# Second FFN: four passes over the input rows on another engine, and the row transposes later in a group

## The chip, the cores and the metric

The kernel runs on one core of a Trainium2 chip. The metric is device time in microseconds (us), the median over several executions. A profiled execution gives the trace: for each engine (PE for matmuls, DVE for vector work, ACT for activations and copies, POOL for GpSimd, SP for DMA issue) every instruction with its start and duration, counted from the first instruction of the execution.

## The reference

Sixteen batches of 256 rows of width 256 go through two layers. Each layer adds an attention-like part and a feed-forward part to the rows, each on layer-normalised rows. The change touches only the last of the four, an FFN with simulated 4-bit numbers:

```python
def fake_quant_nvfp4(x, global_scale):        # blocks of 16 along the last axis
    amax = jnp.max(jnp.abs(xb), axis=-1, keepdims=True)
    sc8 = jnp.clip(amax / 6.0 * global_scale, 0.0, 448.0).astype(float8_e4m3fn)
    dq = sc8 / global_scale
    a = jnp.clip(jnp.abs(xb) / safe_dq, 0.0, 6.0)
    q = jnp.sign(xb) * _FP4_VALS[jnp.digitize(a, _FP4_MIDS)]
    return (q * dq).reshape(sh)
...
gate_out = nvfp4_linear(x, gate_w, s_in[0])   # both operands quantised, then a matmul
up_out = nvfp4_linear(x, up_w, s_in[0])
hidden = jax.nn.silu(gate_out) * up_out       # 1024 wide
return nvfp4_linear(hidden, down_w, s_in_down[0])
```

So both the normalised rows (256 wide) and the hidden activations (1024 wide) are scaled by block, clamped, rounded and multiplied back before a matmul.

## The kernel before, in words

The 4096 rows are 32 tiles of 128 rows (a row is a partition). The second FFN takes them in 8 groups of four tiles. Each engine has its own instruction list, written out by hand, and the engines meet in semaphores. Work on three groups is in flight at once. In one round of the DVE list, `group(g, rows)` (L2226), DVE does, in this order:

- `rows_sizes(g + 2)`: the largest value of each block of 16 of the input rows two groups ahead, from a copy `absx` that ACT made (L1930, L1932);
- `hidden_sizes(g)`: the same for the hidden activations of group g (L1959, L1961, L1930, L1932);
- `block_scales`: five small instructions on 320 columns, 64 for rows and 256 for hidden, ending in a reciprocal (L1936 to L1941). They write `inv16` (what to multiply by before rounding) and `scb` (what to multiply by after);
- the four passes over the 1024 row elements of a partition: `rows_scaled` (L1965, times `inv16`, into `xf`), `clamped` (L1973), `rounded` (L1976) and the last multiplication into `xq` (L1981), which tells `s_xq`;
- the four passes over the first half of the hidden activations (2048 elements each: L1970, L1973, L1976, L2215), and then, in turn, the second half's passes and `product` (L2223, one instruction for each half of a tile: SiLU of the gate times the up result, PSUM and SBUF in, `hh` out) for the four tiles of group g + 1.

Rounds 0 to 5 handle rows (for groups 2 to 7); round 6 and the closing group have none. The rows of groups 0 and 1 are quantised before the rounds.

PE, in `finished(i)` (L1506), first transposes the quantised rows of group i + 2 (`x_in`, L1449, into PSUM bank 0), then the hidden activations of group i (`hidden_in`, L1479, in bank 6, 0, 6, 6 for the four tiles), waiting before the second for ACT to have emptied bank 0 (`s_xqe`), and multiplies them by the down weights (`down`, L1495 and L1497). Then `ahead(i + 1)` (L1500) does gate (L1458) and up (L1467) for the four tiles of group i + 2; `up` waits for `product` to free its banks.

ACT, in its `group(i)` (L1021), does SiLU (L988), a 16-bit copy of the hidden activations (`hidden_half`, L996), then `x_out` (L980, bank 0 to `xqT`), two of the `hidden_out` copies (L1012), `tile_norm(i + 4)` for i up to 3 (six instructions, L824 to L829: normalise four tiles, make `absx` and `xb`), the other two `hidden_out` and a `result` (L1017).

POOL has nothing to do in the second FFN. Earlier it issues indirect DMAs and does two-input multiplications and additions in 32-bit floats (among them L592 and L629).

`Steps.link(ins)` in the listing lets an instruction raise a semaphore and makes the same engine wait for it, before the next instruction reads the result.

Of the kernel before, what the change touches and what calls it, by code (L numbers as in the profile page):

```python
# [7 lines left out]
ALU = mybir.AluOpType  # L8
# [6 lines left out]
I16 = mybir.dt.int16  # L15
U32 = mybir.dt.uint32

P = 128
# [44 lines left out]
def two_layers_kernel(nc, x, itok, ctxT, ctxO, mask, maskT, w_redT, wgT, W1, W2, b2,  # L63
# [46 lines left out]
    with es:  # L110
# [3 lines left out]
        def sem(name):  # L114
            return es.enter_context(nc.semaphore(name))

        def sem2(name):
            return [sem(f"{name}{h}") for h in range(2)]
# [279 lines left out]
                             "s_dn", "s_y")]  # L398
        s_h, s_gs, s_nm2, s_x4 = sem("s_h"), sem("s_gs"), sem("s_nm2"), sem("s_x4")
        s_ax, s_ah = sem("s_ax"), sem("s_ah")  # L400
        s_out = sem2("s_out")
        N_CONST = 12

# [113 lines left out]
        def _(pool):  # L517
# [100 lines left out]
            def weight_scaled(k, first=False):  # L618

                if not first:  # L620
                    pool.wait_ge(s_wp, k)
                pool.sem_inc(s_idle, 1)
                flat = wraw[:].rearrange("p n d -> p (n d)")
                src = (flat[:, 0:2 * FT * D][:, bass.ds(k * NGU, NGU)].rearrange("p (t k b) -> p t k b", t=TGU, k=BLOCK),
                       wraw[:, 2].rearrange("p (t k b) -> p t k b", t=DC, k=BLOCK)[:, :, :, bass.ds(k * BDN, BDN)])
                inv = (wblk[:, 4, 0:2 * NWB // 3][:, bass.ds(k * (NGU // BLOCK), NGU // BLOCK)].rearrange("p (t b) -> p t b", t=TGU),
                       wblk[:, 4, 2 * NWB // 3:NWB].rearrange("p (t b) -> p t b", t=DC)[:, :, bass.ds(k * BDN, BDN)])
                for to, x, m in zip((wt[:, 0:NGU], wt[:, NGU:NGU + NDN]), src, inv):
                    ins = pool.tensor_tensor(to.rearrange("p (t k b) -> p t k b", t=x.shape[1], k=BLOCK), x,  # L629
                                             m.unsqueeze(2).broadcast_to([P, m.shape[1], BLOCK, m.shape[2]]), ALU.mult)  # L630
                ins.then_inc(s_wm, 1)
# [43 lines left out]
            with pool.Else():  # L675
                pool.sem_inc(s_cv, 1)
                with pool.Fori(0, NB) as b:
                    pool.wait_ge(s_cv, b + 1)
                    pool.tensor_copy(cb[:], ctxs[:, bass.ds(b, 1), :, 0:S].rearrange("p o c s -> p (o c) s")).then_inc(s_cb, 1)
                pool.wait_ge(s_cv, NB + 1)  # L680
                weight_first()
                for k in range(1, SLOTS):
                    weight_scaled(k)


        @block.scalar
        def _(act):
# [132 lines left out]
            def tile_norm(g, g0):  # L820

                for u in range(4):
                    t = g * 4 + (u + 1)
                    ins = act.activation(x4s[g0 % 2][:, u * D:(u + 1) * D], X2[:, bass.ds(t, 1), 0:D].rearrange("p o d -> p (o d)"), ACT.Identity,  # L824
                                         bias=nm2[:, bass.ds(t, 1)], scale=rs2[:, bass.ds(t, 1)])
                ins.then_inc(s_x4, 1)
                act.wait_ge(s_x4, g + 1)
                act.activation(absx[g0 % 2], top(x4s[g0 % 2]), ACT.Abs)
                act.copy(xb[g0 % 2], top(x4s[g0 % 2])).then_inc(s_ax, 1)  # L829
# [164 lines left out]
            def hidden_half(t, u):  # L994
                act.wait_ge(s_h, 2 * t + 2)
                act.copy(hb[:, u * FF:(u + 1) * FF], upper(u)).then_inc(s_ah, 1)  # L996
# [13 lines left out]
            def hidden_out(g, u, banks=(6, 0, 6, 6)):  # L1010
                act.wait_ge(s_hT, g * 4 + (u + 1))
                act.copy(hqT[:, u % 2].rearrange("p c t -> p (c t)"), bank[banks[u]][:].bitcast(BF16)).then_inc(s_hTe, 1)  # L1012

            def result(g, k):
                act.wait_ge(s_dn, g * 4 + (2 * k + 2))
                act.wait_ge(s_out[k], g * 16 + 16)
                act.activation(yo[:, k].rearrange("p t d -> p (t d)"), bank[(1, 7)[k]][:], ACT.Copy, scale=gmx[:, 10:11]).then_inc(s_y, 2)  # L1017
# [3 lines left out]
            def group(i):  # L1021
                t = i * 4 + 4
                last = i == NGR - 2
                if i == 0:
                    x_out(1)
                silu(t, 0)
                silu(t + 1, 1)
                if i:
                    result(i - 1, 1)
                hidden_half(t, 0)  # L1030
                silu(t + 2, 2)
                hidden_half(t + 1, 1)
                silu(t + 3, 3)
                hidden_half(t + 2, 2)
                hidden_half(t + 3, 3)
                if not last:
                    x_out(i + 2)
                hidden_out(i, 0)
                hidden_out(i, 1)
                if i + 4 < NGR:  # L1040
                    tile_norm(i + 4, i + 4)
                hidden_out(i, 2)
                hidden_out(i, 3)
                result(i, 0)

            for i in range(NGR - 1):
                group(i)
# [6 lines left out]
        def _(pe):  # L1054
# [390 lines left out]
            def x_in(g):  # L1445
                pe.wait_ge(s_xq, g + 1)
                for u in range(4):
                    for c in range(DC):
                        ins = pe.transpose(bank[0][:].bitcast(BF16)[:, (u * DC + c) * P:(u * DC + c + 1) * P],  # L1449
                                           xq[g % 2][:, u, c * P:(c + 1) * P], identb[:])  # L1450
                ins.then_inc(s_xqT, 1)
# [31 lines left out]
            def down(i, u, turn=False, banks=(1, 7)):  # L1483
                pe.wait_ge(s_hTe, i * 4 + (u + 1))
                if turn:
                    hidden_in(i, 3)
                rows = banks[0] == 1
                if u == 0:
                    if rows:
                        pe.wait_ge(s_y, i * 4)  # L1490
                    else:
                        pe.wait_ge(s_h, 2 * NTILE)
                to = bank[banks[u // 2]][:, (u % 2) * D:(u % 2 + 1) * D]
                if rows:
                    pe.matmul(to, ones[:], X2[:, bass.ds(i * 4 + (u + 1), 1), 0:D].rearrange("p o d -> p (o d)"), start=True, stop=False)  # L1495
                for c in range(FT):
                    ins = pe.matmul(to, hqT[:, u % 2, c, :], dT[:, c, :], start=not rows and c == 0, stop=c == FT - 1)  # L1497
                ins.then_inc(s_dn, 1)
# [5 lines left out]
                    up(i * 4 + (4 + u), u)  # L1504

            def finished(i):  # L1506
                if i + 2 < NGR:
                    x_in(i + 2)
                hidden_in(i, 0)
                if i + 2 < NGR:  # L1510
                    pe.wait_ge(s_xqe, i + 3)
                hidden_in(i, 1)
                down(i, 0)
                hidden_in(i, 2)
                down(i, 1)
                down(i, 2, turn=True)
                down(i, 3)

# [15 lines left out]
        def _(v):  # L1534
# [422 lines left out]
            def hidden_sizes(g, steps):  # L1957
                v.wait_ge(s_ah, g * 4 + 3)
                ts(absh[:, 0:3 * FF].bitcast(I16), hb[:, 0:3 * FF].bitcast(I16), 0x7FFF, None, ALU.bitwise_and)  # L1959
                v.wait_ge(s_ah, g * 4 + 4)  # L1960
                steps.link(ts(absh[:, 3 * FF:].bitcast(I16), hb[:, 3 * FF:].bitcast(I16), 0x7FFF, None, ALU.bitwise_and))  # L1961
                halves(absh, halfh, 4, NBH // 4, big[:, hid_c], steps)
# [263 lines left out]
            def group(g, rows):  # L2226

                t = g * 4 + 4
                later = g > 0
                if rows:  # L2230
                    rows_sizes(g + 2, g + 2, st)
                hidden_sizes(g, st)
                block_scales(slice(0 if rows else NBX, NBX + NBH), st)
                if rows:
                    rows_scaled(g + 2, st)
                    rows_quantised(g + 2, st)
                hidden_scaled(0, st)
                st.need()
                clamped(hf[:, pair[0]], st)
                rounded(hf[:, pair[0]], st)  # L2240
                if later:
                    v.wait_ge(s_hT, g * 4 - 2)
                hidden_quantised(0)
                product(t, 0)
                hidden_scaled(1, st)
                product(t + 1, 1)
                st.need()
                clamped(hf[:, pair[1]], st)
                rounded(hf[:, pair[1]], st)
                product(t + 2, 2)  # L2250
                if later:
                    v.wait_ge(s_hT, g * 4)
                hidden_quantised(1)
                product(t + 3, 3)
# [109 lines left out]
```

## Time and profile before

| what | us |
|---|---|
| median of 3 runs | 712.79 (712.4 to 712.82) |
| profiled execution, device time | 713.3 |
| its span, first to last instruction | 711.1 |
| PE busy | 567.0 (80%) |
| DVE busy | 504.9 (71%) |
| ACT busy | 378.0 (53%) |
| POOL busy | 213.3 (30%) |

The busy times are shares of the whole span, over stages that differ: the second FFN is the part from about 505 us to the end. The profiled execution took 2.2 us more than its span and 0.5 us more than the median. A view by time gives, for a stretch, how long each engine worked in it; the trace in order of time gives, for each instruction, its start, its duration, its line, and in brackets how long its engine had been idle and who ended that.

### The profile page before, as it was taken

To read this page: it belongs to the slowest core of one execution; us is meant where nothing else is said; L and a number is where in the kernel's file an instruction comes from. 1 tells how busy PE (TensorE), PEld (TensorE's weight loads), DVE (VectorE), ACT (ScalarE), POOL (GpSimd) and SP (SyncE) were. 2 spreads that over 40 slices of the span, in tenths; PEclk is the share of its full clock that TensorE was granted. 3 is DMA by queue.
4 is the path that set the end of the run, shared out by engine and by line. 5 is a ranking of instruction groups with operands and counts; after the bars stand their busy time and mean duration, and the time that the engine had idled before them with its cause. 6 is when DMAs were issued, how large, how long until landed. Compare 5 with 4: busy or idle time off the path is not lost.

```text
span 711.1 us, 14550 instructions
## 1 busy us (share of the span) xinstructions
PE 567.0 (80%) x4543; PEld 417.5 (59%) x4552; DVE 504.9 (71%) x1418; ACT 378.0 (53%) x717; POOL 213.3 (30%) x243
## 2 busy tenths in 40 slices
PE   5399999609999999966899999996435865778777
PEld 3188888409998998954566666664212443345445
DVE  6358787694655566673556777663769999999987
ACT  1324443113443333324667777767675878785674
POOL 5724774514655455652222333310000000000000
PEclk9689999959999999996999999999667999998899
DMA  8873443269466655607000000000000000000001
GB/s 318 270 229 117 131 150 116 76 221 386 140 221 198 198 177 181 202 29 238 2 1 0 0 0 0 0 2 1 4 1 0 30 15 16 30 29 16 16 30 60
DMA packets 35540, 68.49 MB, mean 96 GB/s; under 512 B 5581, under 2 KB 24542, under 8 KB 34464
## 3 DMA queue, kind: packets, MB, share of 16 engines
q1 hardware_dynamic: 28816, 52.37, 22.4%
q0 software_dynamic: 5520, 13.61, 5.5%
q10 hardware_dynamic: 1152, 1.88, 0.8%
q8 instruction: 26, 0.43, 0.2%
q14 instruction: 26, 0.21, 0.1%
HBM read 53.78 MB, written 15.80 MB: 98 GB/s over the span
## 4 chain that ended last, share of the span: by engine, by line
PE 45%; DVE 22%; ACT 13%; issue 8%; DMA 7%; SPq 3%; POOL 2%; DVEq 0%; POOLq 0%; ACTq 0%
PE quad L1118 10%; PE quad L1183 5%; DVE hh L2223 5%; ACT nPT L869 4%; PE bank L1192 4%; PE bank L1254 3%; PE quad L1467 3%; PE quad L1273 2%; DMA x_after_ffn<-row,niU 2%; PE quad L1296 2%; DVE nM L2069 2%; DMA early<-in_W 2%; ACT hqT L1012 2%; DMA X<-x_after_ffn 2%; PE duo L1307 2%
## 5 line engine op out<-in xcount | busy, mean ns | idle before, releaser
L777 ACT ACTIVATE hid<-quad,early 128x128 f32<-128x128 f32 x156 | 44.6, 369 | 83.5 <-PE quad L1183 83.5
L1183 PE MATMUL quad<-xts,early 128*128 128x128 f32 x624 | 75.4, 280 | 3.5 <-DMA early<-in_W 3.4
L1183 PEld LDWEIGHTS quad<-xts,early 128*128 128x128 f32 x624 | 73.5, 195 | 6.0 <-issue 4.0
L1192 PE MATMUL bank<-W2s,hid 128*128 x312 | 70.5, 379 | 0.0
L1192 PEld LDWEIGHTS bank<-W2s,hid 128*128 128x128 f32 x312 | 57.8, 190 | 7.1
L598 POOL DMA_INDIRECT x_after_ffn<-row,niU x39 | 39.1, 1002 | 57.4 <-DVE row L1849 40.4
L1467 PE MATMUL quad<-uT,xqT 128*128 128x512 bf16 x128 | 39.7, 414 | 17.5 <-DVE hh L2223 16.5
L988 ACT ACTIVATE sil<-quad,gmx 128x512 f32<-128x512 f32 x64 | 41.1, 688 | 20.5 <-PE quad L1458 20.0
L1844 DVE SCALAR_TENSOR_TENSOR row<-bank,sco,row 128x256 f32<-128x256 f32 x39 | 18.6, 476 | 45.9 <-PE bank L1192 45.4
L2069 DVE TENSOR_REDUCE nM<-quad 128x32 f32<-128x2048 f32 x16 | 36.7, 2292 | 18.6 <-PE quad L1273 18.6
L2223 DVE SCALAR_TENSOR_TENSOR hh<-quad,gmx,sil 128x512 f32<-128x512 f32 x64 | 45.1, 744 | 4.8 <-PE quad L1467 4.3
L564 POOL DMA_INDIRECT rows_by_expert<-row,pi x38 | 37.9, 996 | 33.8 <-DVE pi L1686 23.1
L557 POOL DMA_INDIRECT xg<-in_x,idxu x38 | 37.1, 975 | 28.9 <-DVE lgt L1642 11.5
L1458 PE MATMUL quad<-gT,xqT 128*128 128x512 bf16 x120 | 35.0, 413 | 12.5 <-ACT xqT L980 12.0
L1118 PE MATMUL quad<-ctxs,hid 128*128 x160 | 41.8, 418 | 2.2 <-issue 2.2
L996 ACT COPY wraw<-hh 128x1024 bf16<-128x1024 bf16 x32 | 33.5, 1047 | 17.6 <-DVE hh L2223 17.2
L1118 PEld LDWEIGHTS quad<-ctxs,hid 128*128 128x128 f32 x160 | 31.6, 203 | 10.6 <-issue 4.1
L1254 PE MATMUL bank<-xt,WqS 128*128 128x256 f32 x128 | 36.4, 414 | 1.3 <-ACT xt L854 1.3
L1467 PEld LDWEIGHTS quad<-uT,xqT 128*128 128x128 bf16 x128 | 10.0, 103 | 44.9 <-DVE hh L2223 37.3
L1930 DVE TENSOR_TENSOR ctxs<-ctxs 128x512 bf16<-128x512 bf16 (+4 forms) x48 | 26.2, 546 | 14.1 <-ACT ctxs L829 12.8
L2091 DVE TENSOR_TENSOR X<-bank,X 128x512 f32<-128x512 f32 (+1 forms) x16 | 11.1, 692 | 34.9 <-PE bank L1318 19.7
L1118 PE MATMUL quad<-ctxs,xts 128*128 x144 | 34.9, 395 | 0.0
(365 smaller groups left out, 1326.4 us busy)
## 6 DMA issues: line engine op xcount, KB each, us to landing
early<-in_W SPq DMA_DIRECT2D x37, 514.0 KB, 5.6
row<-rows_by_expert SPq DMA_DIRECT2D x38, 134.0 KB, 2.3
early<-in_ctxO SPq DMA_DIRECT2D x4, 1024.0 KB, 8.0
ctxs<-in_ctxT SPq DMA_DIRECT2D x4, 1024.0 KB, 13.7
W2s<-in_W SPq DMA_DIRECT2D x8, 512.0 KB
X<-x_after_ffn SPq DMA_DIRECT2D x7, 516.0 KB, 7.4
out<-yo SPq DMA_DIRECT2D x14, 256.0 KB, 2.1
early<-in_W ACTq DMA_DIRECT2D x2, 514.0 KB, 8.5
```

The source lines that it names most:

```text
L557: pool.indirect_dma_start(xg[g % NXG][:, u, :], None, x, bass.IndirectOffsetOnAxis(ap=idxu[:, 4 * g + u:4 * g + u + 1], axis=0)).then_inc( ...
L564: pool.indirect_dma_start(rows_d, bass.IndirectOffsetOnAxis(ap=pi[:, g % 3, u:u + 1], axis=0), row[g % 3][:, u, :], None, bounds_check=E2 ...
L598: pool.indirect_dma_start(x2_d, bass.IndirectOffsetOnAxis(ap=niU[:, h, u:u + 1], axis=0), row[h][:, u, 0:XW], None, bounds_check=NT - 1, o ...
L777: ins = act.activation(hid[:, u, c * P:(c + 1) * P], bank[2 + u][:, c * P:(c + 1) * P], ACT.Gelu, bias=W1r[:, k, DC * H2 + c:DC * H2 + c + 1])
L988: act.activation(sil[:, u % 2, k * 512:(k + 1) * 512], bank[2 + k][:], ACT.Silu, scale=gmx[:, 8:9]).then_inc(s_sil, 1)
L1118: ins = pe.matmul(quad[:, u, 0:CW], xz[g % 2][:, u, z, c, :], ctxs[:, bass.ds(ex, 1), c, :].rearrange("p o s -> p (o s)"), start=z + c == ...
L1183: ins = pe.matmul(bank[2 + u][:, n * P:(n + 1) * P], W1r[:, m % RING, c * H2 + n * P:c * H2 + (n + 1) * P], xt[:, u, c, :], start=c == 0, ...
L1192: ins = pe.matmul(bank[6 + u % 2][:, 0:D], hid[:, u, c * P:(c + 1) * P], W2s[:, bass.ds(ex, 1), c, :].rearrange("p o s -> p (o s)"), start ...
L1254: ins = pe.matmul(bank[6][:, n * S:(n + 1) * S], WqS[:, c, n * P:(n + 1) * P], xt3[:, c, :], start=c == 0, stop=c == DC - 1)
L1467: ins = pe.matmul(bank[4 + k][:], xqT[:, u, c, :], uT[:, c, k * 512:(k + 1) * 512], start=c == 0, stop=c == DC - 1)
L2069: red(nM[:].rearrange("p k q m -> p k (q m)"), quad[:].rearrange("p k (n s) -> p k n s", s=KW), AX.X, ALU.max).then_inc(n_rd, 1)
L2223: v.scalar_tensor_tensor(hh[u // 2][:, o:o + 512], bank[4 + k][:], gmx[:, 11:12], sil[:, u % 2, k * 512:(k + 1) * 512], ALU.mult, ALU.mult ...
```

## The change

The four passes over the rows two groups ahead leave DVE and go to POOL's list, for groups 2 to 7. POOL waits for `s_psc`, a new semaphore that DVE raises after `block_scales`, and for the quantised rows of the group before. DVE's `block_scales`, which overwrites the scales, now waits until POOL has finished with the last ones (`s_xq`). On PE, `x_in(i + 2)` moves from the head of `finished(i)` to the place between `down(i, 1)` and `down(i, 2)`, and the wait for bank 0 before `hidden_in(i, 1)` goes. On ACT, `x_out(i + 2)` moves behind the third `hidden_out`, and `tile_norm(i + 4)` moves to the end of the group, with a wait until POOL has finished the rows of group i + 2. The rows of groups 0 and 1 stay on DVE.

```diff
+        s_psc = sem("s_psc")
...
+            def rows_quantised(g):
+                cells = xf.rearrange("p (t k b) -> p t k b", t=16, k=BLOCK)
+
+                def each(a):
+                    a = a[:, 0:NBX].rearrange("p (t b) -> p t b", t=16)
+                    return a.unsqueeze(2).broadcast_to([P, 16, BLOCK, a.shape[2]])
+
+                pool.wait_ge(s_psc, g - 1)
+                pool.wait_ge(s_xq, g)
+                st.link(pool.tensor_tensor(cells, xb[g % 2].rearrange("p (t k b) -> p t k b", t=16, k=BLOCK), each(inv16), ALU.mult))
+                st.link(pool.tensor_scalar(xf, xf, FP4_MAX * FINE, -FP4_MAX * FINE, ALU.min, ALU.max))
+                st.link(pool.tensor_scalar(xf.bitcast(I16), xf.bitcast(I16), GRID, GRID, ALU.add, ALU.subtract))
+                pool.tensor_tensor(xq[g % 2][:].rearrange("p u d -> p (u d)").rearrange("p (t k b) -> p t k b", t=16, k=BLOCK), cells,
+                                   each(scb), ALU.mult).then_inc(s_xq, 1)
+
+            for g in range(2, NTILE // 4):
+                rows_quantised(g)
...
                 hidden_half(t + 3, 3)
+                hidden_out(i, 0)
+                hidden_out(i, 1)
+                hidden_out(i, 2)
                 if not last:
                     x_out(i + 2)
-                hidden_out(i, 0)
-                hidden_out(i, 1)
-                if i + 4 < NGR:
-                    tile_norm(i + 4, i + 4)
-                hidden_out(i, 2)
                 hidden_out(i, 3)
                 result(i, 0)
+                if i + 4 < NGR:
+                    act.wait_ge(s_xq, i + 3)
+                    tile_norm(i + 4, i + 4)
...
             def finished(i):
-                if i + 2 < NGR:
-                    x_in(i + 2)
                 hidden_in(i, 0)
-                if i + 2 < NGR:
-                    pe.wait_ge(s_xqe, i + 3)
                 hidden_in(i, 1)
                 down(i, 0)
                 hidden_in(i, 2)
                 down(i, 1)
+                if i + 2 < NGR:
+                    x_in(i + 2)
                 down(i, 2, turn=True)
                 down(i, 3)
...
                 hidden_sizes(g, st)
+                if rows:
+                    v.wait_ge(s_xq, g + 2)
                 block_scales(slice(0 if rows else NBX, NBX + NBH), st)
                 if rows:
-                    rows_scaled(g + 2, st)
-                    rows_quantised(g + 2, st)
+                    v.sem_inc(s_psc, 1)
                 hidden_scaled(0, st)
```

## Rows read from the trace of the kernel before

**Rows 1.** Busy time by stretch; the stretches are DVE's rounds 0, 2 and 6.

```profile
core 0: us, PE busy (x) PEld busy (x) DVE busy (x) ACT busy (x) POOL busy (x), PEclk, DMA share, GB/s
524.44:548.50 24.06, 13.21 (x47) 5.15 (x48) 23.10 (x35) 13.16 (x18) 0.00 (x0) 0.63 0.00 0
...
572.21:595.93 23.72, 16.09 (x111) 9.29 (x112) 23.00 (x37) 19.00 (x25) 0.00 (x0) 1.00 0.07 23
...
667.08:689.52 22.44, 18.39 (x111) 11.19 (x112) 19.40 (x28) 14.75 (x19) 0.00 (x0) 0.85 0.07 24
```

**Rows 2.** DVE in order of time, round 2: start, duration, engine, line, operation.

```profile
572.21 1.00 DVE L1930 TENSOR_TENSOR ctxs<-ctxs 128x512 bf16<-128x512 bf16 x3
...
580.83 0.69 DVE L1965 TENSOR_TENSOR ctxs<-ctxs 128x1024 f16<-128x1024 bf16 x1
581.55 0.43 DVE L1973 TENSOR_SCALAR ctxs<-ctxs 128x1024 f16<-128x1024 f16 x1
...
583.08 1.22 DVE L1970 TENSOR_TENSOR hf<-wraw,ctxs 128x2048 f16<-128x2048 bf16 x1
584.33 0.69 DVE L1973 TENSOR_SCALAR hf<-hf 128x2048 f16<-128x2048 f16 x1
...
585.79 1.23 DVE L2215 TENSOR_TENSOR hq<-hf,ctxs 128x2048 bf16<-128x2048 f16 x1
586.93 1.40 DVE L2223 SCALAR_TENSOR_TENSOR hh<-quad,gmx,sil 128x512 f32<-128x512 f32 x2
...
595.93 1.00 DVE L1930 TENSOR_TENSOR ctxs<-ctxs 128x512 bf16<-128x512 bf16 x3
```

**Rows 3.** POOL and DVE in order of time, one stretch of the first FFN.

```profile
287.77 2.36 POOL L592 TENSOR_TENSOR row<-xts,row 128x1024 f32<-128x1024 f32 x1 [0.18 <-POOL xts L587]
...
287.96 0.45 DVE L1844 SCALAR_TENSOR_TENSOR row<-bank,sco,row 128x256 f32<-128x256 f32 x1
...
289.48 0.70 DVE L1795 TENSOR_TENSOR dl<-row,lmx 128x32 f32<-128x32 f32 x1
```

**Rows 4.** All instructions of line L1795: durations in ns, min, median, max.

```profile
L1795 DVE TENSOR_TENSOR dl<-row,lmx x10: 191/328/704, 158.2 to 289.5; 128x32 f32<-128x32 f32 x10
```

**Rows 5.** POOL and DVE in order of time, two stretches of the second attention.

```profile
401.59 1.76 POOL L629 TENSOR_TENSOR ctxs<-wraw,ctxs 128x512 f32 x2 [0.39 <-ACT ctxs L813]
...
402.57 0.18 DVE L2076 CAST nMb<-nM 128x32 bf16<-128x32 f32 x1
...
402.79 0.60 DVE L2077 TENSOR_TENSOR nMr<-nM,nMb 128x32 f32<-128x32 f32 x1
...
411.04 1.74 POOL L629 TENSOR_TENSOR ctxs<-wraw,ctxs 128x512 f32 x2 [0.24 <-issue]
...
412.17 0.64 DVE L2076 CAST nMb<-nM 128x32 bf16<-128x32 f32 x1
```

**Rows 6.** POOL's instructions by line and shape, whole span: count, busy us, mean ns.

```profile
L592 POOL TENSOR_TENSOR row<-xts,row 128x1024 f32<-128x1024 f32 x10 | 23.6, 2363 | 1.8 <-POOL xts L587 1.8
...
L522 POOL TENSOR_SCALAR_AFFINE_SELECT before<-ones 128x128 f32<-128x128 f32 x1 | 0.3, 293 | 0.1
...
L545 POOL TENSOR_SCALAR_AFFINE_SELECT ownh<-ones 128x8 f32<-128x8 f32 x1 | 0.2, 208 | 0.0
```

**Rows 7.** ACT and PE in order of time, round 2.

```profile
572.33 1.04 ACT L996 COPY wraw<-hh 128x1024 bf16<-128x1024 bf16 x1 [1.40 <-DVE hh L2223]
...
574.18 1.01 ACT L1012 COPY hqT<-bank 128x1024 bf16<-128x1024 bf16 x1
...
575.99 2.08 ACT L824 ACTIVATE ctxs<-X,nm,rs 128x256 f32<-128x256 f32 x4
...
580.00 1.00 ACT L1012 COPY hqT<-bank 128x1024 bf16<-128x1024 bf16 x1
...
584.83 1.27 ACT L988 ACTIVATE sil<-quad,gmx 128x512 f32<-128x512 f32 x2 [1.50 <-PE quad L1458]
...
576.66 0.61 PE L1479 MATMUL bank<-identb,hq 128*128 128x128 bf16 x8
```

## What the rows say of the change, before it ran

> **What bounds the kernel now.** I read the busy times by stretch first, cut at the starts of DVE's rounds [rows 1]. In a full round DVE works 23.00 of 23.72 us, PE 16.09, ACT 19.00, POOL nothing. Round 0 takes 24.06, rounds 1 to 5 take 23.71 or 23.72 (one of the five stands there), and round 6, which has no input rows, 22.44 with only 19.40 of work. Then I read DVE in order of time through one full round [rows 2]: no instruction in it has idle time in front; the 0.7 us that are missing are the hand-overs of a few hundredths between instructions. So in rounds 0 to 5 DVE sets the pace, and anything that lengthens or shortens its list moves the end, up to where another engine comes last. Last I looked for stretches earlier in the kernel where POOL and DVE work side by side [rows 3, 4, 5], since in the second FFN they never do.
>
> **What leaves DVE.** The four passes start at 580.83 and the next instruction starts at 583.08 [rows 2]: 2.25 us a round, six rounds, 13.5 us. Nothing else on DVE gets shorter. The added wait and the added raise are sequencer steps; if the raise costs like the hand-overs above, a few hundredths, it is inside the rounding.
>
> **What the passes cost on POOL.** No row of before has POOL working on 16-bit rows, so I go by the nearest. A two-input multiplication of 1024 elements takes 2.36 us [rows 6]; 768 elements in two broadcast multiplications take 1.76, which is 2.29 ns an element and again 2.35 us for 1024 [rows 5]. I take 2.36 for the first and the last pass. From below, if POOL's time went by bytes, half of it, 1.18. For the two one-input passes the nearest rows are a select over 8 elements, 208 ns, and over 128, 293 ns [rows 6]: 0.71 ns an element, so 208 + 1016 x 0.71 = 930 ns. From above, they could be as slow as the two-input ones, 2.36. I take 0.93, because these selects too read one input. The four together: 2.36 + 0.93 + 0.93 + 2.36 = 6.6 us.
>
> The Trainium skill (GPSIMD Engine Reference, section 4.1, Engine selection) calls one-input work on GpSimd roughly line-rate and two-input work about twice as slow as on the Vector engine. No row here shows a one-input pass of this size; at one element a cycle of the 1.2 GHz that the Trainium skill gives there, 1024 elements would be an estimated 0.85 us, which would make the sum below 1 us smaller over six rounds.
>
> **Is POOL late?** It may start when `block_scales` ends, 8.6 us into a round (580.83 less 572.21, [rows 2]). Its result is wanted by PE in the next round, behind two `down`, and by DVE before the next `block_scales`, 5.4 us into it. With a round of 21 to 27 us that leaves 18 us or more for 6.6 us of work. The new waits of DVE, PE and ACT on POOL should therefore be found already satisfied, unless POOL is held up threefold; at zero I cost them.
>
> **What POOL costs DVE.** This is the term that decides. In the first FFN POOL adds 1024 elements from 287.77 to 290.13. A two-input DVE instruction of 32 elements starts in it at 289.48 and lasts 0.70 us, to 290.18, just past POOL's end [rows 3]; the same line's shortest is 0.19 [rows 4]. In the second attention POOL's pair of multiplications ends at 403.35, and a two-input DVE instruction that started at 402.79 ends at 403.39; the next pair ends at 412.78, and a one-input cast from 412.17 ends at 412.81, 0.64 us where it otherwise takes 0.18 [rows 5]. So while POOL reads, DVE's two-input instructions stand still until it is done, and a one-input one can too. But an instruction with one input in PSUM and one in SBUF takes its usual 0.45 us inside POOL's 2.36 [rows 3]. `product` is of that kind.
>
> Of the 16-bit clamp and rounding passes on DVE no row stands beside POOL. Their speed tells what they use: from 1024 to 2048 elements a clamp grows by 0.26 us and a two-input pass by 0.53 [rows 2]. The clamp thus reads as many elements per us through one operand as the other through two, and I take it that it needs both ways into the memory and is held like it. (The cast at 412.17 is a one-input instruction that is.)
>
> The Trainium skill (SBUF — State Buffer, section Who interferes with whom) states this as a rule: Vector instructions with two SBUF inputs or in a two-port mode share a port pair with GpSimd, whoever starts first has it for the whole instruction, and the other stands still. The rows above agree for two-input instructions (0.70 for 0.19 us); for the clamp no run here shows it yet. By the rule the sum is the one that follows; if only two-input instructions were held, it would be that of the second rival below.
>
> Who gets in when both wait? At 402.57 POOL is between its two multiplications, DVE does a cast of 0.18, and the next DVE instruction, 0.04 later, finds POOL already inside and is held for 0.4 us [rows 5]. So a waiting POOL instruction gets in at the hand-over between two DVE instructions. I expect them to alternate: DVE's `hidden_scaled(0)` runs (1.22); POOL's first pass gets in behind it and holds DVE's clamp 2.36; the clamp runs while POOL waits for its own semaphore; POOL's second pass holds the rounding 0.93; its third holds `hidden_quantised(0)` 0.93; its fourth gets in behind that and lies over the first two `product` (1.40, free), so that it holds `hidden_scaled(1)` only 2.36 - 1.40 = 0.96. Sum: 2.36 + 0.93 + 0.93 + 0.96 = 5.18 us a round. From above, with one-input passes at 2.36: 8.04. From below, with two-input passes at 1.18 and the last wholly covered: 3.04; that a held instruction makes part of its own start-up while it waits (0.51 lost of 0.65 overlap at 289.48, [rows 3, 4]) is inside that.
>
> **What the new order is worth.** On PE and ACT, `x_out` and `tile_norm` (4.01 us, from 575.99 to 580.00, [rows 7]) leave the front of the chain that feeds the `down` matmuls. While DVE is the bound that gives nothing: DVE wants the first SiLU 12.5 us into a round at the earliest, 14.7 today less 2.25, and later still when it is held. In round 6 DVE has 22.44 - 19.40 = 3.0 us without work [rows 1], and there `x_out` no longer stands before the first `hidden_out`: at most one copy of 0.93 less, against eight more transposes in the path. I take 0 for it, with 0.5 either way.
>
> **Sum.** A round: 23.72 - 2.25 + 5.18 = 26.65, so 2.93 longer; six rounds, 17.6 us. The profiled execution took 713.3, so 730.9, and 0.5 less for the median: **730 us**, 2.5% slower. Its bounds: 3.04 - 2.25 = 0.79 a round gives 717.5; 8.04 - 2.25 = 5.79 gives 747.5.
>
> **Rivals.**
>
> *No holding worth the name: faster.* POOL's 16-bit passes might read too little, or too briefly, to stop DVE. Then DVE's round is 21.47 and ACT comes last in rounds 1 to 4: from the end of the last `product`, 0.12, then six copies at 0.93 (572.33 to 574.18 holds two), a `result` like a SiLU instruction at 0.64, `tile_norm` 4.01, the first SiLU 0.64, and the wait for PE before the third `hidden_out`: its transposes come 2.48 behind the start of the first [rows 7], so 1.3 after the second ends. That is 12.3, up to 13.6 with such a wait before `x_out` as well; then 9.0 from the first `product` to the round's end [rows 2]. Some 22.1: gain 1.6 in four rounds, 2.25 in rounds 0 and 5, 10.9 us: 702. It decides once the holding is under 2.25 us a round. Against it speak the rows on which the sum rests.
>
> *DVE keeps POOL out: no change.* If a DVE list without gaps wins every hand-over, POOL gets in only beside `product`: pass 1 beside the first two (holds 0.96), passes 2 and 3 beside later ones (nothing), pass 4 beside the last two (0.96 into the next round). 1.92 against 2.25: gain 0.3 a round, 2 us: 711. The case that only two-input instructions are held comes to the same: 0.9 for the first pass behind clamp and rounding, 0.9 for the third. The hand-over at 402.57 speaks against it.
>
> *TensorE cools down in the longer rounds.* The granted clock was 1.00 in round 2 and 0.63 in round 0, where PE had 13.2 of 24.06 us of work [rows 1]; 0.63 mixes the level 2.4 GHz with 1.2. If rounds of 26.65 us run at 1.2 throughout, PE's 16.09 us become up to 32 and its chain from the first `hidden_out` to the first `up` outlasts DVE by some 2 us a round: 742. For it: round 6 had 0.85 with 3 us of waiting. Against it: only part of each round fell so far.
>
> **Chances.** Alternation 0.70 (717.5 to 747.5 by itself), no holding 0.10, DVE keeps POOL out 0.12, cooler TensorE 0.08. Within 0.2% (1.4 us) is about what a measurement of this kernel can tell from no change. Faster than that: the first rival and half the second, 0.16. Within it: the other half, 0.06. Slower: the rest, 0.78. A range without the second rival holds under 8 in 10, so it goes from 710 to 748.
>
> **What the profile after would show.** Rounds of about 26.7 us. DVE's L1973 on 2048 elements at 3.0 instead of 0.69 for the first half, L1976 at 1.6, L2215 at 2.1, the second L1970 at 2.2; L2223 still at 0.74. POOL with four instructions a round, 6.6 us together if nothing holds it, finished some 10 us after `block_scales`. No DVE idle before `block_scales`, no PE idle before L1449 that POOL ends. The prediction is wrong if DVE's passes keep their durations beside POOL's (first rival), if POOL's passes begin only at L2223 (second), if a one-input pass takes 2 us (size, 740 and more), or if POOL comes later than 18 us after its start, so that DVE waits for it outright.

## The result, and the profile after

The changed kernel took 727.34 us (median of 4 runs, 725.07 to 728.39) against 712.81 for the kernel before on the same chip: a ratio of 1.0194, 95% interval 1.0174 to 1.0215. The forecast was 730 us in a range of 710 to 748, slower with 0.78. The profiled execution took 726.89 us, its span 725.2; before it was 713.3 and 711.1.

First the busy times by stretch, columns as in [rows 1], cut at the starts of DVE's rounds 0, 2 and 6 (PEclk is the clock granted to PE as a share of its full one, 2.4 GHz):

```profile
526.01:552.22 26.21, 12.34 (x47) 4.45 (x48) 25.48 (x31) 13.27 (x18) 9.68 (x4) 0.65 0.00 0
578.42:604.60 26.18, 19.30 (x111) 10.46 (x112) 25.45 (x32) 19.08 (x25) 9.67 (x4) 0.87 0.06 21
...
683.16:703.21 20.05, 15.78 (x111) 9.42 (x112) 19.32 (x28) 14.70 (x19) 0.00 (x0) 1.00 0.08 27
```

DVE has fewer instructions in a round (32 for 37) and is busy for longer: 25.45 us of 26.18, where it was 23.00 of 23.72 [rows 1]. POOL works 9.67 us a round. Round 6, where POOL has nothing to do, is 2.4 us shorter than before, at a granted clock of 1.00 for 0.85 (e1 comes back to it). The reason for the longer rounds is in the order of time; this is POOL and DVE in round 2, from the last instruction of `block_scales` on:

```profile
584.84 2.15 DVE L1959 RECIPROCAL ctxs<-ctxs 128x320 f16<-128x320 f32 x1
587.13 1.92 POOL L695 TENSOR_TENSOR ctxs<-ctxs 128x1024 f16<-128x1024 bf16 x1 [16.26 <-DVEq L2255]
587.14 2.98 DVE L1988 TENSOR_TENSOR hf<-wraw,ctxs 128x2048 f16<-128x2048 bf16 x1
589.14 1.89 POOL L696 TENSOR_SCALAR ctxs<-ctxs 128x1024 f16<-128x1024 f16 x1
590.16 1.41 DVE L1991 TENSOR_SCALAR hf<-hf 128x2048 f16<-128x2048 f16 x1
591.11 3.95 POOL L697 TENSOR_SCALAR ctxs<-ctxs 128x1024 int16<-128x1024 int16 x1
591.61 1.40 DVE L1994 TENSOR_SCALAR hf<-hf 128x2048 int16<-128x2048 int16 x1
593.05 1.23 DVE L2233 TENSOR_TENSOR hq<-hf,ctxs 128x2048 bf16<-128x2048 f16 x1
594.19 1.41 DVE L2241 SCALAR_TENSOR_TENSOR hh<-quad,gmx,sil 128x512 f32<-128x512 f32 x2
595.14 1.92 POOL L698 TENSOR_TENSOR xq<-ctxs 128x1024 bf16<-128x1024 f16 x1
595.51 2.63 DVE L1988 TENSOR_TENSOR hf<-wraw,ctxs 128x2048 f16<-128x2048 bf16 x1
598.06 1.40 DVE L2241 SCALAR_TENSOR_TENSOR hh<-quad,gmx,sil 128x512 f32<-128x512 f32 x2
```

L695 to L698 are the four passes on POOL. L1988, L1991, L1994, L2233 and L2241 of this kernel are L1970, L1973, L1976, L2215 and L2223 of before. Two more rows of before, from the same round as [rows 2], are the rounding and the second half's scaling:

```profile
585.06 0.69 DVE L1976 TENSOR_SCALAR hf<-hf 128x2048 int16<-128x2048 int16 x1
...
588.25 1.21 DVE L1970 TENSOR_TENSOR hf<-wraw,ctxs 128x2048 f16<-128x2048 bf16 x1
```

Read each DVE duration against its row of before: scaling 2.98 for 1.22, clamp 1.41 for 0.69, rounding 1.40 for 0.69, the second half's scaling 2.63 for 1.21 to 1.22. That is 1.76 + 0.72 + 0.71 + 1.41 = 4.60 us a round that DVE lost beside POOL's passes. The last multiplication (L2233) kept its 1.23 although L697 was still running, and the pair of `product` its 1.41. The gap between the reciprocal's end (586.99) and the next DVE instruction is 0.15 us; in e5 (below), which has no raise of `s_psc`, it is 0.03 (577.41 + 2.15, then 579.59). So a round became 4.60 + 0.12 - 2.25 = 2.47 us longer. From one round to the next it is 26.19 where it was 23.71: 2.48.

POOL is done at 597.06, 10 us after `block_scales`, and in the list of waits from 526 us on no engine waits for it.

The bridge, from profile to profile: rounds 0 to 5 are 14.5 us longer, round 6 2.4 shorter, the closing group 0.4 longer, and the first round starts 1.6 us later (526.01 for 524.44): 14.1 of span. The 1.6 us arise ahead of the code that the change touches. The point in round 0 where the 3072 columns of hidden sizes start lies at 525.7 before, 527.3 after, and between 523.7 and 528.2 in the nine experiments, whose earlier stages are the same code, so I give it no cause.

### The profile page after: what moved, and what is told of

Read it like the earlier page. It is cut to its first block, busy times and chain, and to the rows that moved or that the text cites. A ratio compares the mean times of both kernels' runs of the same rounds, so it can differ in the third digit from the quotient of the medians.

```text
span 725.2 us, 14562 instructions
## 1 busy us (share of the span) xinstructions
PE 574.7 (79%) x4543; PEld 417.2 (58%) x4552; DVE 519.9 (72%) x1394; ACT 378.0 (52%) x717; POOL 271.4 (37%) x267
## 4 chain that ended last, share of the span: by engine, by line
PE 41%; DVE 30%; issue 9%; ACT 9%; DMA 7%; SPq 3%; POOL 2%; DVEq 0%; POOLq 0%; ACTq 0%
PE quad L1138 10%; PE quad L1203 5%; DVE hh L2241 5%; ACT nPT L888 4%; PE bank L1212 4%; PE bank L1274 3%; DVE ctxs L1948 3%; PE quad L1487 3%; DVE hf L1988 2%; DMA x_after_ffn<-row,niU 2%; PE quad L1293 2%; DMA early<-in_W 2%; PE quad L1316 2%; DVE nM L2087 2%; DVE ctxs L1959 2%
## 5 line engine op out<-in xcount | busy, mean ns | idle before, releaser
L695 POOL TENSOR_TENSOR ctxs<-ctxs 128x1024 f16<-128x1024 bf16 x6 | 11.5, 1917 | 146.8 <-DVEq L2255 146.8
L1487 PE MATMUL quad<-uT,xqT 128*128 128x512 bf16 x128 | 42.8, 445 | 23.5 <-DVE hh L2241 22.8
L1478 PE MATMUL quad<-gT,xqT 128*128 128x512 bf16 x120 | 38.7, 445 | 19.8 <-ACT xqT L999 12.0
L2241 DVE SCALAR_TENSOR_TENSOR hh<-quad,gmx,sil 128x512 f32<-128x512 f32 x64 | 45.0, 743 | 2.7 <-PE quad L1487 2.3
L1988 DVE TENSOR_TENSOR hf<-wraw,ctxs 128x2048 f16<-128x2048 bf16 x15 | 37.4, 2492 | 0.9
L1478 PEld LDWEIGHTS quad<-gT,xqT 128*128 128x128 bf16 x128 | 13.4, 112 | 40.3 <-ACT xqT L999 12.1
```

What stands on the lines that cost most here:

```text
L1478: ins = pe.matmul(bank[2 + k][:], xqT[:, u, c, :], gT[:, c, k * 512:(k + 1) * 512], start=c == 0, stop=c == DC - 1)
L1487: ins = pe.matmul(bank[4 + k][:], xqT[:, u, c, :], uT[:, c, k * 512:(k + 1) * 512], start=c == 0, stop=c == DC - 1)
L1988: steps.put(tt(blocks(hf[:, pair[p]], 2), blocks(hb[:, pair[p]], 2), each_block(inv16[:, pair_c[p]], 2), ALU.mult))
L2241: v.scalar_tensor_tensor(hh[u // 2][:, o:o + 512], bank[4 + k][:], gmx[:, 11:12], sil[:, u % 2, k * 512:(k + 1) * 512], ALU.mult, ALU.mult ...
```

## The experiments

Theory: while POOL reads its operands from SBUF, DVE's instructions with two SBUF inputs, and its one-input 16-bit passes, stand still, and nothing else in the change costs time. Main rival: the new order of `x_in`, `x_out` and `tile_norm` does it. In what follows "round" is the time from the start of a round's 3072-column instruction to that of the next (23.7 us before, 26.2 after).

**e1, the order alone.** The passes stay on DVE; PE and ACT have the new order.

```diff
...
+                hidden_out(i, 2)
                 if not last:
                     x_out(i + 2)
...
+                if i + 4 < NGR:
+                    act.wait_ge(s_xq, i + 3)
+                    tile_norm(i + 4, i + 4)
...
```

> The new order on PE and ACT alone; the four passes stay on DVE. Theory (each side's share is separate: the order is worth round 6 and nothing else): rounds 1 to 5 stay at 23.7 us, round 6 goes from 22.4 to 20.1, in all 2.4 us less than before, some 710.4. Rival 1 (round 6 of the changed kernel was short only because the longer rounds before it gave PE and ACT a lead): round 6 stays at 22.4, 712.8. Rival 2 (the late normalisation keeps SiLU waiting and so lengthens the rounds 1 to 4): 24 us or more in those, 714 or more.

Measured: 714.38 us (12 runs, 710.12 to 716.37) against 712.99, ratio 1.002 (1.0005 to 1.0035). Rounds 0 to 5 stayed at 23.7; round 6 came to 21.61. Its row, as in [rows 1]:

```profile
668.31:689.92 21.61, 17.40 (x112) 10.37 (x112) 19.43 (x29) 14.65 (x19) 0.00 (x0) 0.92 0.07 25
```

The order doesn't lengthen the rounds. Round 6 lies between theory (20.1) and rival (22.4), and the granted clock goes with it; the 710.4 us that the theory expected were missed. The run e7 (below), whose PE and ACT lists are those of the changed kernel, shows it best; its round 6:

```profile
682.88:705.70 22.82, 18.61 (x112) 11.07 (x112) 19.41 (x28) 14.65 (x19) 0.00 (x0) 0.85 0.07 24
```

Put together from such rows of all kernels:

| PE's and ACT's order in round 6 | granted clock | round 6, us |
|---|---|---|
| before's: before, e2 | 0.85 | 22.44 |
| new: e4, e7, e9 | 0.85 | 22.81, 22.82, 22.94 |
| new: e1, e3, e5, e6, e8 | 0.92 | 21.60 to 21.61 |
| new: the changed kernel | 1.00 | 20.05 |

At the same clock, 0.85, the new order is 0.4 us slower, not faster. The 2.4 us that the changed kernel's profile shows in round 6 are the clock that PE found there in that execution, with 15.8 us of matmuls for 18.4. Finer stretches of round 6 show where e7 and the changed kernel part:

```profile
684.38:690.38 6.00, 5.37 (x24) 3.91 (x25) 5.69 (x11) 2.50 (x3) 0.00 (x0) 0.50 0.01 3
...
684.66:690.66 6.00, 5.38 (x54) 4.67 (x54) 5.69 (x11) 4.01 (x5) 0.00 (x0) 1.00 0.01 3
```

In e7 (above) the clock is 0.50 there, which is 1.2 GHz, and PE gets 24 matmuls done where the changed kernel (below), at 2.4 GHz, does 54. In both PE had just waited 2.94 us for ACT at the head of the round. What decides whether the clock falls is open: the two have the same order and rounds of the same length. So the order has no gain of its own that these runs show.

**e2, the passes alone.** The four passes on POOL, with PE's and ACT's order of before (ACT's wait before `tile_norm` stays).

```diff
+                if not last:
+                    x_out(i + 2)
                 hidden_out(i, 0)
                 hidden_out(i, 1)
+                if i + 4 < NGR:
+                    act.wait_ge(s_xq, i + 3)
+                    tile_norm(i + 4, i + 4)
                 hidden_out(i, 2)
...
+                if i + 2 < NGR:
+                    x_in(i + 2)
                 hidden_in(i, 0)
+                if i + 2 < NGR:
+                    pe.wait_ge(s_xqe, i + 3)
                 hidden_in(i, 1)
...
```

> The four passes on GpSimd alone; the order on PE and ACT is that of before. Theory (holding of DVE alone makes the rounds longer): rounds 26.2 us as in the changed kernel, round 6 back at 22.4, in all 15 us more than before, some 727.7 to 729.7. Rival (part of the longer rounds comes from the new order, say the normalisation in front of SiLU): rounds under 25.5, 723 or less.

Measured: 727.55 us (4 runs), ratio 1.0192 (1.0169 to 1.0214), and in round 2:

```profile
579.30:605.48 26.18, 19.05 (x112) 10.59 (x112) 25.45 (x32) 19.14 (x25) 9.67 (x4) 0.87 0.06 21
```

The same 26.18 and the same 25.45 of DVE as in the changed kernel. The passes on POOL make the whole loss; the order has no part in it that shows.

**e3, POOL by itself.** DVE waits after its raise until POOL has finished, so nothing runs beside the passes on DVE.

```diff
                     v.sem_inc(s_psc, 1)
+                    v.wait_ge(s_xq, g + 3)
```

> The changed kernel, but DVE stands still from its raise until GpSimd has finished the four passes, so that neither disturbs the other. Theory (the times listed for GpSimd's two one-input passes, 1.89 and 3.96, are in good part waiting behind DVE): two-input passes 1.9 each as before, clamp about 0.9, rounding 1 to 2; all DVE passes at 1.22, 0.69, 0.69, 1.22, 1.21; rounds 21.6 + 5.7 to 6.7 + small gaps, 27.5 to 28.5. Rival (the listed times are GpSimd's own work): 1.89 and 3.96 again, rounds of 31.5.

Measured: one run, 752.47 us. POOL and DVE in order of time, round 1:

```profile
563.92 1.91 POOL L695 TENSOR_TENSOR ctxs<-ctxs 128x1024 f16<-128x1024 bf16 x1 [21.61 <-DVEq L2255]
565.92 1.04 POOL L696 TENSOR_SCALAR ctxs<-ctxs 128x1024 f16<-128x1024 f16 x1
567.04 3.63 POOL L697 TENSOR_SCALAR ctxs<-ctxs 128x1024 int16<-128x1024 int16 x1
570.75 1.91 POOL L698 TENSOR_TENSOR xq<-ctxs 128x1024 bf16<-128x1024 f16 x1
572.70 1.23 DVE L1988 TENSOR_TENSOR hf<-wraw,ctxs 128x2048 f16<-128x2048 bf16 x1 [8.92 <-POOL xq L698]
```

These are the true prices: 1.91, 1.04, 3.63, 1.91, together 8.5 us. The clamp's 1.89 beside DVE is 1.04 of work and 0.85 of waiting behind L1988. The rounding pass is 3.63 by itself, three and a half times the clamp on as many elements, and yet it held DVE for only 0.71. The theory was right on the clamp (about 0.9) and wrong on the rounding pass (1 to 2), so the rounds, 30.4 us, met neither expectation (27.5 to 28.5, and 31.5).

**e4, the first pass twice.** One more pass of 1.91 us on POOL in each round.

```diff
+                st.link(pool.tensor_tensor(cells, xb[g % 2].rearrange("p (t k b) -> p t k b", t=16, k=BLOCK), each(inv16), ALU.mult))
```

> The changed kernel with GpSimd's first pass done twice (the same result again). Theory (a GpSimd instruction that gets in costs DVE its own length): the second copy holds DVE's clamp for 1.9 instead of the 0.7 that the one-input pass held it, and the rest moves one place back; rounds 1.9 to 2.6 longer than 26.2, so 28.1 to 28.8, in all 11 to 16 us over the changed kernel. Rival 1 (a fixed price for each GpSimd instruction, by semaphores and hand-overs, 4.6 over four): rounds 27.3. Rival 2 (GpSimd's work goes into time that DVE has to spare): 26.2.

Measured: one run, 733.34 us; rounds of 26.77, 0.58 longer than after, between the two lowest of the three expectations; none of them was right. POOL and DVE, round 2:

```profile
588.81 2.98 DVE L1989 TENSOR_TENSOR hf<-wraw,ctxs 128x2048 f16<-128x2048 bf16 x1
590.80 2.78 POOL L696 TENSOR_TENSOR ctxs<-ctxs 128x1024 f16<-128x1024 bf16 x1
591.83 2.29 DVE L1992 TENSOR_SCALAR hf<-hf 128x2048 f16<-128x2048 f16 x1
...
594.16 1.41 DVE L1995 TENSOR_SCALAR hf<-hf 128x2048 int16<-128x2048 int16 x1
...
595.60 1.94 DVE L2234 TENSOR_TENSOR hq<-hf,ctxs 128x2048 bf16<-128x2048 f16 x1
597.46 1.40 DVE L2242 SCALAR_TENSOR_TENSOR hh<-quad,gmx,sil 128x512 f32<-128x512 f32 x2
598.78 1.21 DVE L1989 TENSOR_TENSOR hf<-wraw,ctxs 128x2048 f16<-128x2048 bf16 x1
599.14 2.63 POOL L699 TENSOR_TENSOR xq<-ctxs 128x1024 bf16<-128x1024 f16 x1
...
601.23 1.08 DVE L1992 TENSOR_SCALAR hf<-hf 128x2048 f16<-128x2048 f16 x1
```

The second copy holds the clamp 1.60, and everything behind it moves one place: the rounding pass now reads beside L2234 (1.94 for 1.23), and the last pass comes after the second half's scaling has begun, which keeps 1.21 instead of 2.63, and reaches past `product` to hold the second half's clamp 0.40 (1.08 for 0.68). The sum is 1.76 + 1.60 + 0.72 + 0.71 + 0.40 = 5.19, which is 0.59 more than 4.60, as in the rounds (0.58). So a pass of 1.91 us more cost 0.58: what POOL's passes cost is set by what stands beside them, not by their length alone.

**e5, the passes beside `product`.** If that is so, POOL's passes should be cheap beside `product`, which reads PSUM. POOL waits for the first half's last multiplication (`s_hq`), its rounding for the first half of the third `product`, its last pass for the second half's last multiplication; DVE's raise goes.

```diff
-                pool.wait_ge(s_psc, g - 1)
+                pool.wait_ge(s_hq, 2 * g - 3)
...
+                pool.wait_ge(s_h, 8 * g - 4 + 1)
                 st.link(pool.tensor_scalar(xf.bitcast(I16), ...
+                pool.wait_ge(s_hq, 2 * g - 2)
...
-                if rows:
-                    v.sem_inc(s_psc, 1)
```

> The changed kernel with the same four passes on GpSimd, started at other points of DVE's list: the first when the first half's last multiplication is done (so beside the first product), the rounding behind the first half of the third product, the last behind the second half's last multiplication (beside the fourth product). DVE's raise goes. Theory (what a pass costs is what lies beside it; product is not held): the first pass holds the second half's scaling for 0.6, the clamp nothing, the rounding 0.2, the last pass the next round's first instruction 0.6; 1.4 to 1.6 instead of 4.7 a round against 2.25 saved, rounds of 22.9 to 23.2, in all 705 to 709. Rival 1 (the passes cost their 4.6 wherever they lie): rounds of 26. Rival 2 (GpSimd is now late for PE and for DVE's next scales): DVE idle before its scales, rounds over 24.

Measured: 715.04 us (12 runs) against 712.93, ratio 1.0039 (1.002 to 1.0057); rounds of 24.26, one of 25.46 (in which DVE is idle 1.74 us for a SiLU). POOL and DVE, round 2:

```profile
582.31 1.23 DVE L2235 TENSOR_TENSOR hq<-hf,ctxs 128x2048 bf16<-128x2048 f16 x1
583.61 1.92 POOL L695 TENSOR_TENSOR ctxs<-ctxs 128x1024 f16<-128x1024 bf16 x1 [12.04 <-DVE hq L2235]
583.78 1.41 DVE L2243 SCALAR_TENSOR_TENSOR hh<-quad,gmx,sil 128x512 f32<-128x512 f32 x2 [0.25 <-ACT sil L1009]
585.11 1.50 DVE L1990 TENSOR_TENSOR hf<-wraw,ctxs 128x2048 f16<-128x2048 bf16 x1
...
590.20 3.63 POOL L698 TENSOR_SCALAR ctxs<-ctxs 128x1024 int16<-128x1024 int16 x1 [2.69 <-DVE hh L2243]
590.62 1.70 DVE L2235 TENSOR_TENSOR hq<-hf,ctxs 128x2048 bf16<-128x2048 f16 x1
592.24 1.40 DVE L2243 SCALAR_TENSOR_TENSOR hh<-quad,gmx,sil 128x512 f32<-128x512 f32 x2
593.56 2.68 DVE L1950 TENSOR_TENSOR ctxs<-ctxs 128x512 bf16<-128x512 bf16 x3
```

The placement took 1.9 of the 2.5 us back, but not more. Held are L1990 by 0.28, L2235 by 0.48, and the next round's first maxima by 1.68 (2.68 for 1.00, [rows 2]): the last pass waits for the end of the 3.63 us at 593.83 and falls on them instead of on `product`. And DVE idles 0.25 us for a SiLU. 23.71 - 2.25 + 0.28 + 0.48 + 1.68 + 0.25 = 24.15, of 24.26 measured. The theory's 22.9 to 23.2 was missed. Rounds over 24 were the second rival's, but not for its reason: DVE has no idle time before its scales.

**e6, two passes that only write.** First and last pass are replaced by memsets of the same tiles: the scaling and the last multiplication of the rows of groups 2 to 7 are left out.

```diff
-                st.link(pool.tensor_tensor(cells, xb[g % 2]... each(inv16), ALU.mult))
+                st.link(pool.memset(xf, 0.25))
...
+                pool.memset(xq[g % 2][:].rearrange("p u d -> p (u d)"), 0.25).then_inc(s_xq, 1)
```

> The changed kernel with GpSimd's first and last pass replaced by fills of the same 1024 elements, which read nothing (scaling and last multiplication are left out). Theory (DVE's two-input instructions are held by GpSimd's reading): the first half's scaling 1.22 instead of 2.98 and the second half's 1.22 instead of 2.63; clamp and rounding of the first half still held, by up to 1.0 each; rounds of 23.0 to 23.5. Rival (any work of GpSimd holds them, reading or writing, for its length): the two still held by the 0.9 to 1.0 that a fill of this size takes; rounds of 24.5 to 25.

Measured: one run, 712.18 us; rounds of 23.01 (round 0), then 23.75. POOL and DVE, round 2:

```profile
581.62 0.95 POOL L695 MEMSET ctxs<- 128x1024 f16 x1 [16.55 <-DVEq L2254]
581.65 1.23 DVE L1987 TENSOR_TENSOR hf<-wraw,ctxs 128x2048 f16<-128x2048 bf16 x1
...
582.91 1.41 DVE L1990 TENSOR_SCALAR hf<-hf 128x2048 f16<-128x2048 f16 x1
...
587.69 0.75 DVE L2240 SCALAR_TENSOR_TENSOR hh<-quad,gmx,sil 128x512 f32<-128x512 f32 x1 [0.66 <-ACT sil L1006]
```

A POOL instruction that only writes costs a two-input DVE instruction nothing (1.23), while the clamp, which reads, still holds 0.72. So it is POOL's reading that holds a two-input instruction; a fill beside one of DVE's one-input 16-bit passes doesn't occur in these rounds. The durations are those of the theory, but the rounds behind round 0 are longer than its 23.0 to 23.5: again DVE, once it is faster, waits for ACT.

**e7, the rounding pass on floats.** The third pass reads and writes the same 16 bits as f16 instead of int16, so the rows of groups 2 to 7 are rounded wrongly; the work is the same in size.

```diff
-                st.link(pool.tensor_scalar(xf.bitcast(I16), xf.bitcast(I16), GRID, GRID, ALU.add, ALU.subtract))
+                st.link(pool.tensor_scalar(xf, xf, GRID, GRID, ALU.add, ALU.subtract))
```

> The changed kernel with GpSimd's rounding pass done on the same bytes read as 16-bit floats instead of 16-bit integers (a wrong rounding, the same amount of data). Theory (the 3.6 us of that pass by itself come from the integers, and most of them hold nobody): the pass takes 1.0 and holds DVE's rounding 0.7 as before; the last pass comes 2.5 us earlier and now holds the last multiplication of the first half for 1.8 instead of the next scaling for 1.4; rounds 26.2 to 26.8 although GpSimd works 2.6 us less. Rival (DVE loses by GpSimd's working time): rounds 2.6 us shorter, 23.6.

Measured: one run, 729.04 us; the pass took 3.95 us beside DVE, as in the changed kernel, and rounds 26.19. Both expectations built on the type, and the type isn't it. That leaves the pair of operations (add and subtract against min and max), which I didn't try by itself.

**e8, e9: the two things that e5 showed.** In e8 the rounding pass starts straight behind the clamp, so that the last pass comes earlier. In e9, besides, `tile_norm` stands behind the second `hidden_out` again, as before the change.

```diff
# e8, against e5
-                pool.wait_ge(s_h, 8 * g - 4 + 1)
# e9, against e8
                 hidden_out(i, 1)
+                if i + 4 < NGR:
+                    act.wait_ge(s_xq, i + 3)
+                    tile_norm(i + 4, i + 4)
                 hidden_out(i, 2)
...
                 result(i, 0)
-                if i + 4 < NGR:
-                    act.wait_ge(s_xq, i + 3)
-                    tile_norm(i + 4, i + 4)
```

> The passes beside product as in the run before (e5), but the rounding pass starts straight behind the clamp instead of 2.7 us later, so that the last pass lies beside the last two product instructions and not on the next round's rows_sizes. Theory (only what lies beside an instruction with two SBUF inputs, or a fast 16-bit one, costs DVE): the 1.68 us that L1950 lost at the head of a round fall to about 0.5, rounding's reading costs 0 to 0.7 on the second half's clamp, so DVE's own list is 23.0 to 23.3 us a round; the end 707 to 709. Rival: ACT's chain with tile_norm in front of the SiLU has become the bound at 23.7 to 24.3 us, so DVE idles before the first product of a round for what it saves; rounds stay at 23.7 to 24.3, the end 711 to 715.

> As e8, and tile_norm stands behind the second hidden_out on ACT again, as in the kernel before; x_in and x_out stay in the new places. If ACT's chain is the bound in e8 (rival there), tile_norm now fills the 2.6 us in which ACT waits for PE before the third hidden_out, the first SiLU of a round comes 1 to 2.5 us sooner, DVE no longer idles before product, and rounds come to 22.9 to 23.3; the end 706 to 709, below before. If ACT was not the bound, rounds are those of e8 within 0.1. Against a gain: the third and fourth hidden_out come up to 1.4 us later, and with them down and the gate matmuls, so the first SiLU may come no sooner.

Measured, e8: 712.72 us (12 runs) against 713.31, ratio 0.9992 (0.9967 to 1.0018), rounds of 23.9 (23.4 for round 0). ACT and DVE, round 2:

```profile
577.72 1.01 ACT L1032 COPY hqT<-bank 128x1024 bf16<-128x1024 bf16 x1 [2.45 <-PE bank L1500]
...
582.32 2.08 ACT L844 ACTIVATE ctxs<-X,nm,rs 128x256 f32<-128x256 f32 x4
...
584.30 1.23 DVE L2234 TENSOR_TENSOR hq<-hf,ctxs 128x2048 bf16<-128x2048 f16 x1
...
587.04 1.41 DVE L2242 SCALAR_TENSOR_TENSOR hh<-quad,gmx,sil 128x512 f32<-128x512 f32 x2 [1.51 <-ACT sil L1008]
```

DVE saves time and stands 1.51 us before `product`, for the SiLU that comes behind `tile_norm`; the rival was right. ACT itself had idled 2.45 us for PE before the third `hidden_out`.

Measured, e9: **710.10 us** (12 runs, 707.84 to 714.21) against 713.31, ratio 0.9951 (0.9928 to 0.9974): faster than both kernels, by 0.5% against the one before; the expected 706 to 709 was just missed. ACT, POOL and DVE, rounds 2 and 3:

```profile
573.98 2.08 ACT L844 ACTIVATE ctxs<-X,nm,rs 128x256 f32<-128x256 f32 x4
...
582.91 1.26 ACT L1008 ACTIVATE sil<-quad,gmx 128x512 f32<-128x512 f32 x2 [1.50 <-PE quad L1479]
...
584.26 1.40 DVE L2242 SCALAR_TENSOR_TENSOR hh<-quad,gmx,sil 128x512 f32<-128x512 f32 x2
585.58 1.84 DVE L1989 TENSOR_TENSOR hf<-wraw,ctxs 128x2048 f16<-128x2048 bf16 x1
...
588.41 3.63 POOL L697 TENSOR_SCALAR ctxs<-ctxs 128x1024 int16<-128x1024 int16 x1
588.67 1.32 DVE L1992 TENSOR_SCALAR hf<-hf 128x2048 f16<-128x2048 f16 x1
...
594.53 1.69 DVE L1949 TENSOR_TENSOR ctxs<-ctxs 128x512 bf16<-128x512 bf16 x3
```

The first SiLU now waits for PE (1.50) and no longer for ACT's own list, and DVE finds it done: no idle time at 584.26. What is left of the holding is 0.62 (L1989), 0.63 (L1992) and 0.69 (L1949): 23.71 - 2.25 + 1.94 = 23.40, and the rounds are 23.43. The expected rounds of 22.9 to 23.3 left out the first two, in part. Of the 2.25 us that leave DVE, 0.3 a round is won. In the profiled executions the stretch from round 0 to round 6 (between their 3072-column instructions) takes 138.8 us for 141.4, and round 6, whose clock is 0.85 in both, gives 0.5 of that back; that is 2.1 of the 3.2 us between the medians, and the rest I could not place.

## Why the prediction was right, step by step

- **DVE sets the pace in rounds 0 to 5:** right. Each us of holding appeared in the round (2.47 worked out, 2.48 measured), and the bound moved to ACT only when DVE saved more (e6, e8).
- **The cost of holding, 5.18 a round:** the step that was mis-sized, 4.60, with the raise 0.12 beside it. The clamp and the rounding are held, as inferred from their speed on DVE. Alternation is right, but POOL's first pass gets in ahead of `hidden_scaled(0)`, not behind it: the raise leaves DVE 0.15 us, and L695 starts 0.01 before L1988. So each pass holds the instruction one place earlier than forecast: L1988 1.76 (forecast 0), clamp 0.72 (2.36), rounding 0.71 (0.93), L2233 nothing (0.93), the second scaling 1.41 (0.96). Only the rounding's came near. That the sum is off by no more than 0.58 is in part luck: errors of 1.76 and 0.45 up and of 2.79 down cancel in it.
- **POOL's prices:** 16-bit two-input passes take 1.91, inside the bounds of 1.18 and 2.36; the clamp 1.04 (forecast 0.93). The rounding pass took 3.63, outside the bound of 2.36 from above. The prediction had a one-input pass of 2 us as a sign that it was wrong, with 740 us and more; the pass was longer and the time 727, since that sign took it that a pass holds DVE for its whole length. The error cost the forecast little, since the pass holds DVE only in its first part: in e9 it starts at 588.41, and the clamp that is held by 0.63 could have begun again at 589.30, some 0.9 us later. By the Trainium skill (SBUF — State Buffer, section Who interferes with whom) whoever has the port pair that DVE and GpSimd share keeps it for the whole instruction. For the 1.91 us passes the traces agree (DVE's 1.22 became 2.98); for this pass they don't: L2233, with two SBUF inputs, ran in 1.23 us beside its remainder, and there the measurement decides.
- **`product` isn't held:** right, in every run (1.39 to 1.41 for a pair).
- **POOL isn't late:** right; 10 us after `block_scales`, with no wait on it.
- **The new order is worth 0, with 0.5 either way:** right at an equal clock, where round 6 loses 0.4 (22.44 against 22.81). What the step left out is that the granted clock in round 6 can go from 0.85 to 1.00, which in the profiled execution gave 2.4 us; the closing group lost 0.4.
- **The rivals.** *No holding:* refuted by e2. Its price was also wrong: ACT's chain from the last `product` of a round to the first of the next took 14.76 us in e8 (572.28 to 587.04), not 12.3 to 13.6, with 2.45 and 1.20 us of waiting for PE in it, so that with the new order hardly any saving on DVE could have shown. *DVE keeps POOL out:* refuted, POOL starts at the first hand-over; that only two-input instructions are held, its second case, is refuted by the clamp (1.41 for 0.69). *Cooler TensorE:* the granted clock did fall, from 1.00 to 0.87 in round 2, but DVE was busy for 25.45 of 26.18 us, as in e2, so it cost nothing there.
- **The sum.** 730 was 2.7 us above the median: a round 0.46 less (the holding 0.58 less, the raise 0.12 more; 2.8 us over six), round 6 2.4 less by its clock, against 1.6 us more ahead of the stage and smaller terms of both signs.

## What to carry to other kernels

Work that leaves a saturated DVE for POOL isn't free: price it by which DVE instructions it will lie beside, pass by pass, and give it a start that lays it beside those that, like `product`, read one operand from PSUM. When the bound does give way, look at once for the engine that comes last next; here ACT's order, harmless while DVE was the bound, ate the whole gain until `tile_norm` was moved into a wait that ACT had anyway. And the length of a pass on the other engine can say little of its cost: 3.63 us held 0.7.

## What the hardware showed that I had not expected

- An add-and-subtract pass over 1024 16-bit elements took POOL 3.63 us, a min-and-max pass 1.04, with nothing beside either (e3); reading the elements as f16 changed nothing (3.95 beside DVE either way, e7). Why is open.
- The long pass holds DVE for some 0.9 us from when it gets in (588.41 to 589.30, worked out from e9), and a two-input DVE instruction runs at full speed beside the rest (1.23 in the changed kernel).
- With the same order of work, round 6 took 20.05, 21.61 or 22.82 us at a granted clock of 1.00, 0.92 or 0.85, in profiled executions of different kernels; after the same wait of 2.94 us PE ran at 1.2 GHz in one and at 2.4 GHz in another.
- A POOL memset of 0.95 us holds no two-input DVE instruction (1.23 beside it, e6).
- A semaphore raised by DVE's own list costs DVE 0.12 us (a gap of 0.15 for 0.03), and in that gap POOL's waiting instruction gets in first (587.13 against 587.14).
